# Routing and scattering tiles 0 to 15 during attention, into a slot region per expert, with unit slots fetched one by one

## The reference

```python
x = x + xattn(layernorm(x), ctx, Wq, Wk, Wv, Wo, bo)     # 16 heads of 64, 64 keys
# moe, on the 4096 rows xf = layernorm(x):
scores = softmax(xf @ gate_w.T)                          # 8 experts
_, idx = top_k(scores + gate_b, 2)
w = take_along_axis(scores, idx)                         # weight of each chosen expert
h = silu((xf @ w1[e] + b1[e]) * (xf @ w3[e] + b3[e]))    # hidden size 352
oe = h @ w2[e] + b2[e]                                   # per expert e
z = the same expert form with sw1, sw3, sw2              # shared expert, every row
x = x + sum_k w_k * oe[idx_k] + z
```

## Time and profile before

| | |
|---|---|
| median of 3 runs | 773.84 us |
| profiled execution, its own time | 774.89 us |
| its span | 773.1 us |
| TensorE busy | 673.9 us (87%) |
| VectorE / ScalarE / GpSimd busy | 535.4 / 396.8 / 426.0 us |
| granted TensorE clock, mean of the span | 0.951 |
| chain that ended last | PE 75%, DMA 12%, DVE 4%, POOL 4%, issue 3% |

### The profile page before, as it was taken

How to read it: one execution, slowest core, us unless ns; L and a number is a source line. 1 busy time by engine, 2 the same in 40 slices (tenths; PEclk the granted TensorE clock), 3 DMA queues, 4 the chain that set the end, 5 groups by cost and what they waited for, 6 DMA issues and landing times.

```text
span 773.1 us, 16281 instructions
## 1 busy us (share of the span) xinstructions
PE 673.9 (87%) x4635; PEld 633.5 (82%) x4636; DVE 535.4 (69%) x1053; ACT 396.8 (51%) x1287; POOL 426.0 (55%) x532
## 2 busy tenths in 40 slices
PE   4996899999999999486884049999999999999995
PEld 3784789999999998386884049999999999999994
DVE  3884888888888876586886016666666666666678
ACT  3995778778787774175331013443443443434432
POOL 5343765656656554124666743677677677676300
PEclk9997999999999999699998559999999999999998
DMA  8203342222222212599421012444444444446495
GB/s 233 75 1 109 103 151 89 79 73 70 70 71 81 69 49 68 148 328 297 119 72 50 1 51 46 77 72 69 76 72 71 78 68 72 77 88 103 86 385 238
DMA packets 65005, 79.96 MB, mean 103 GB/s; under 512 B 11337, under 2 KB 57906, under 8 KB 64946
## 3 DMA queue, kind: packets, MB, share of 16 engines
q1 hardware_dynamic: 47618, 55.81, 23.1%
q0 software_dynamic: 15744, 18.84, 15.5%
q10 hardware_dynamic: 1584, 4.59, 1.5%
HBM read 49.97 MB, written 29.24 MB: 102 GB/s over the span
## 4 chain that ended last, share of the span: by engine, by line
PE 75%; DMA 12%; DVE 4%; POOL 4%; issue 3%; ACT 1%; SPq 0%; ACTq 0%; POOLq 0%; DVEq 0%
PE ps L1094 62%; DMA slots_scratch<-record,slot 9%; POOL slots_scratch L626 4%; PE ps L1249 4%; PE ps L1177 3%; PE ps L1241 2%; PE ps L1154 2%; DMA wq_sb<-in_L_xattn_Wq 1%; DMA xrow<-xn_scratch,slots 1%; PE ps L1196 1%; PE ps L1167 1%; DVE hmax L864 0%; DVE sums L985 0%; PE ps L1113 0%; ACT prob L702 0%
## 5 line engine op out<-in xcount | busy, mean ns | idle before, releaser
L643 POOL DMA_INDIRECT acc_scratch<-yrow,slots x71 | 111.5, 1570 | 71.9 <-ACT yrow L804 70.8
L804 ACT ACTIVATE yrow<-ps,slots 128x256 f32<-128x256 f32 x71 | 33.7, 474 | 148.2 <-PE ps L1094 148.2
L626 POOL DMA_INDIRECT slots_scratch<-record,slot x64 | 66.1, 1032 | 63.1 <-DMA slots_scratch<-record,slot 34.8
L953 DVE TENSOR_TENSOR uxTl<-ps,uxTh 128x256 fp32r<-128x256 f32 x103 | 43.6, 423 | 79.2 <-ACT uxTh L814 78.6
L1094 PE MATMUL ps<-w13h,uxTh 128*128 x284 | 97.4, 343 | 0.0
L971 DVE TENSOR_TENSOR uv<-ps,b 128x704 f32<-128x704 f32 x71 | 63.3, 891 | 47.6 <-PE ps L1094 47.6
L814 ACT ACTIVATE uxTh<-ps 128x256 fp32r<-128x256 f32 x103 | 38.9, 378 | 106.3 <-PE ps L1241 88.4
L1094 PE MATMUL ps<-w13l,uxTh 128*128 x284 | 91.7, 323 | 0.0
L1094 PE MATMUL ps<-w13h,uxTl 128*128 x284 | 91.3, 321 | 0.0
L1241 PE MATMUL ps<-ident,xrow 128*128 128x128 f32 x206 | 40.6, 279 | 49.3 <-DMA xrow<-xn_scratch,slots 39.4
L636 POOL DMA_INDIRECT xrow<-xn_scratch,slots x71 | 69.5, 979 | 23.1 <-issue 20.7
(11 more groups left out here) (206 smaller groups left out, 2197.9 us busy)
## 6 DMA issues: line engine op xcount, KB each, us to landing
sums<-acc_scratch SPq DMA_DIRECT2D x16, 512.0 KB, 10.8
w_raw<-in_L_ffn_w SPq DMA_DIRECT2D x16, 352.0 KB
xin<-in_x SPq DMA_DIRECT2D x32, 128.0 KB, 2.5
acc_scratch<-yrow ACTq DMA_DIRECT2D x8, 512.0 KB, 2.7
xres<-in_x SPq DMA_DIRECT2D x32, 128.0 KB, 2.4
acc_scratch<-x SPq DMA_DIRECT2D x32, 128.0 KB, 1.9
xn_scratch<-xn SPq DMA_DIRECT2D x32, 128.0 KB, 2.4
xrow<-xn_scratch SPq DMA_DIRECT2D x32, 128.0 KB
```

Of the source, the lines that this page charges most:

```text
L626: pool.indirect_dma_start(slots_dram, bass.IndirectOffsetOnAxis(ap=slot[:, k, t:t + 1], axis=0), record[:, t, k, :], None).then_inc(scat_o ...
L643: pool.indirect_dma_start(acc_dram[u % 2], bass.IndirectOffsetOnAxis(ap=slots[:, u, 0:1], axis=0), yrow[:, m % YRING, :], None, compute_op ...
L804: act.activation(yrow[:, y, :], ps[:, 6 + m % 2, 0:D], ACT.Copy, scale=slots[:, bass.ds(u, 1), 1].bitcast(F32)).then_inc(y_ok, 1)
L953: dve.tensor_tensor(uxTl[:, p, :], ps[:, 0, 0:D], f32(uxTh[:, p, :]), ALU.subtract).then_inc(uxTl_ok, 1)
```

## The change

Routing is done in three groups: tiles 0 to 7, 8 to 15 (`GROUPS`) and 16 to 31 (`REST`). The new function `route(stage, ...)` holds the old chain cut in six stages. For the first two groups one stage is run by VectorE at the end of each of six attention steps (steps 14 to 19 and 22 to 27), with an Exp on ScalarE and nine small products on TensorE (`ranks`, in bank 0) between them. GpSimd scatters one tile's two record groups at the end of each attention step 20 to 35. Only tiles 16 to 31 are routed and scattered after attention.

So that a slot number can be given before the number of rows per expert is known, the table in HBM now has one region of 32 blocks of 128 slots per expert (`BLOCKS = 264`), the running count of each expert is kept in `carry`, and VectorE works out afterwards which block each unit has (`unit_row`). SyncE reads that number with `value_load` and fetches each unit's 128 slots by a DMA of its own (`unit_slots`): the first eight at s = 16 of its loop of the shared stage, behind a wait for all scatters, the other 63 behind the loop. The initial table is written during preparation, and ScalarE waits for it before its first write of A. The bias bo is folded into U by eight one-row products, so GpSimd's addition in each attention step is gone. The zeroing of `yrow` moves from the start to the end of preparation.

```diff
@@ SyncE
+            def unit_slots(u):
+                wait(sp, slots_in[u % RING], 16 * (u // RING))
+                row = sp.value_load(unit_row[0:1, u:u + 1], min_val=0, max_val=(BLOCKS - 1) * P)
+                sp.dma_start(slots[:, u, :], slots_dram[bass.ds(row, P), :]).then_inc(slots_in[u % RING], 16)
             for s in range(4, NA + LAG + 1):
+                if s == NA - 4:
+                    sp.wait_ge(eid_ok, 1)
+                    for half in scat_out:
+                        sp.wait_ge(half, 16 * NT)
+                    for u in range(RING):
+                        unit_slots(u)
...
+            for u in range(RING, NU):
+                unit_slots(u)
@@ GpSimd
-                t = s - 3
-                if has(t, NT):
-                    p = (par + 1) % 2
-                    wait(pool, xres_in[p], before(t) + 16)
-                    pool.tensor_tensor(xres[:, p, :], xres[:, p, :], bo_bc[:, :], ALU.add).then_inc(xb_ok, 1)
...
+            pool.memset(yrow[:, :, :], 0.0).then_inc(zero_ok, 1)
...
             def begin_step(s, par):
                 tile_step(s, par)
+                for g, (a, b) in enumerate(GROUPS):
+                    t = a + s - (b + 6 + STAGES)
+                    if a <= t < b:
+                        pool.wait_ge(slot_ok, g + 1)
+                        for k in range(TOP):
+                            scatter_record(t, k)
...
-            for t in range(NT):
+            pool.wait_ge(slot_ok, len(GROUPS) + 1)
+            for t in range(*REST):
                 for k in range(TOP):
...
             def gather(u):
                 m = (R0 + u) % RING
+                pool.wait_ge(slots_in[u % RING], 16 * (u // RING) + 16)
@@ ScalarE
                 elif kind == "A":
+                    if (j, i) == (0, 0):
+                        act.wait_ge(table_out, 16)
...
             def begin_step(s, par):
+                for g, (a, b) in enumerate(GROUPS):
+                    if s == b + 6 + 1:
+                        act.wait_ge(rt_sub, g + 1)
+                        act.activation(score[:, :, :], marked[:, 0, :, :], ACT.Exp).then_inc(rt_exp, 1)
                 tile_step(s, par)
@@ VectorE
+            def route(stage, g, a, b, marked, mark, score, biased, chosen, v, rank):
+                def best(k):
+                    link(dve.tensor_reduce(v[:, 3, :], biased, AX.X, ALU.max))
+                    link(dve.tensor_tensor(marked[:, 0, :, :], biased, over_e(v[:, 3, :]), ALU.is_ge))
+                    link(dve.tensor_tensor(marked[:, 0, :, :], marked[:, 0, :, :], over_t(pref[:, :]), ALU.mult))
+                    link(dve.tensor_reduce(v[:, 3, :], marked[:, 0, :, :], AX.X, ALU.max))
+                    link(dve.tensor_tensor(mark[:, k, :, :], marked[:, 0, :, :], over_e(v[:, 3, :]), ALU.is_equal))
+                if stage == 0:      # 2 instructions, then ScalarE's Exp
...
+                elif stage == 1:    # sum, reciprocal, scale, bias: 4
...
+                elif stage == 2:
+                    best(0)
+                elif stage == 3:
+                    link(dve.scalar_tensor_tensor(out=biased, in0=mark[:, 0, :, :], scalar=LOWEST, in1=biased,
+                                                  op0=ALU.mult, op1=ALU.add))
+                    best(1)
+                elif stage == 4:
+                    dve.tensor_tensor(chosen[:, 0:n, :], mark[:, 0, :, :], mark[:, 1, :, :], ALU.add).then_inc(chosen_ok, 1)
...
+                else:
+                    link(dve.tensor_tensor(biased, rank[:, 0:n, :], over_t(carry[:, :]), ALU.add))
+                    link(dve.tensor_tensor(carry[:, :], rank[:, n, :], carry[:, :], ALU.add))
+                    link(dve.tensor_tensor(marked, mark, biased.unsqueeze(1).to_broadcast([P, TOP, n, E]), ALU.mult))
+                    link(dve.tensor_reduce(v[:, 4:6, :], marked, AX.X, ALU.add))
+                    dve.tensor_copy(slot[:, :, a:b], v[:, 4:6, :]).then_inc(slot_ok, 1)
@@ TensorE
+            def ranks(bank, chosen, n):
+                pe.matmul(ps[:, bank, 0:(n + 1) * E], tri[:, :], chosen[:, :, :].rearrange("p t e -> p (t e)"), start=True, stop=False,
+                          skip_group_check=True)
+                for t in range(n):
+                    last = pe.matmul(ps[:, bank, (t + 1) * E:(n + 1) * E], ones[:, :], ...
...
+                for g, (a, b) in enumerate(GROUPS):
+                    if s == b + 6 + STAGES - 1:
+                        pe.wait_ge(chosen_ok, g + 1)
+                        pe.wait_ge(xTl_ok, s + 1)
+                        ranks(0, chosen, b - a).then_inc(rank_ok, 1)
```

More of the change, by code:

```diff
@@ L889, in tile_step @@
                     wait(dve, O_ok, t + 1)
-                    wait(dve, xb_ok, t + 1)
+                    wait(dve, xres_in[p], before(t) + 16)
                     wait(dve, x2_out[p], before(t))
@@ L938, in _, with begin_step @@
             dve.wait_ge(pre_act, NPRE)
-            steps(NT, 2, 6, tile_step, begun=0)
+            def begin_step(s, par):
+                tile_step(s, par)
+                for g, (a, b) in enumerate(GROUPS):
+                    stage = s - (b + 6)
+                    if stage == 0 and g == 0:
+                        dve.wait_ge(const_ok, 16)
+                    if stage == STAGES - 1:
+                        dve.wait_ge(rank_copied, g + 1)
+                    if 0 <= stage < STAGES:
+                        route(stage, g, a, b, marked[:, :, :, :], mark[:, :, :, :], score[:, :, :], biased[:, :, :],
+                              chosen[:, :, :], gv[:, :, :], rank[:, :, :])
+            dve.wait_ge(small_in, 80)
+            steps(NT, 2, 6, begin_step, begun=0)
             def unit_step(s, m, routed=None):
@@ L1032, in _ @@
-            dve.tensor_tensor(chosen[:, :, :], first[:, :, :], second[:, :, :], ALU.add).then_inc(chosen_ok, 1)
-            for k, mark in enumerate((first, second)):
-                link(dve.tensor_tensor(mA[:, :, :], mark[:, :, :], score[:, :, :], ALU.mult))
-                link(dve.tensor_reduce(record[:, :, k, 1].bitcast(F32), mA[:, :, :], AX.X, ALU.add))
-            dve.wait_ge(small_in, 96)
-            unit_step(0, 0)
-            dve.wait_ge(rank_ok, 1)
-            rows = v32[:, 4, 0:E]
@@ L1067, in _ @@
+            for stage in range(STAGES - 1):
+                rest(stage)
+            unit_step(0, 0)
+            dve.wait_ge(rank_ok, len(GROUPS) + 1)
+            rest(STAGES - 1)
             dve.wait_ge(hid_one, 2)
             unit_step(1, 1)
[L1070 to L1072 removed]
@@ L1073, in _ @@
-            link(dve.tensor_reduce(passed, big[:, :, :], AX.X, ALU.add))
+            rows, tiles, ends = (sums8[:, i, :] for i in range(3))
+            passed, begun, local, block_no = (units[:, i, :] for i in range(4))
+            link(dve.tensor_tensor(rows, carry[:, :], region[:, :], ALU.subtract))
+            link(dve.tensor_tensor(over_tile[:, :, :], rows.unsqueeze(2).to_broadcast([P, E, NT]),
+                                   tile128[:, :].unsqueeze(1).to_broadcast([P, E, NT]), ALU.is_gt))
@@ L1086, in _, with product @@
             PARTS = ((0, 0), (1, 0), (0, 1))
-            def product(out, stationary, moving, n):
+            def product(out, stationary, moving, n, more=False):
                 last = None
```

247 lines of the change are left out of this document (138 added, 109 removed).

## The result

| | median of the runs | runs | profiled execution |
|---|---|---|---|
| before, beside the changed kernel | 774.31 us | 772.53 to 775.34 (4) | 774.89, span 773.1 |
| changed | 781.92 us | 776.01 to 784.63 (4) | 776.01, span 774.3 |

The ratio is 1.0083 (95% interval 1.0051 to 1.0116): slower by 0.8%, where a gain of some 25 us, to 749 us, had been forecast. In a later group ten runs of the changed kernel gave 778.73 us, ratio 1.0054 (1.0025 to 1.0084). Ratios and their intervals leave out two executions in a slower state of the chip, one of 1049.2 us in the first edit of experiment 8 and one of 780.17 us in the second.

What follows compares the result with a forecast made beforehand. TensorE was taken to bound attention, routing and scatters the path after it. 774.89 - 37.5 (gap) + 10.2 (attention) + 2.1 (preparation) = 749.7, predicted as 749; range holding 8 of 10: 739 to 765 us.

Steps and rivals of the forecast that it cites:

- starting 5.8 us early gains about one pair: Behind attention: the 32 remaining scatters start 5.8 us earlier and have all landed at 400, before 419.9, so the gap goes.
- Rival 3: Late slots: scatters keep the first five's 2.98 us each, 32 end at 423, residual row 25 us late, 772; chance 0.14.
- attention's 12: Delay forecast up to the end of attention: 10.2 us in attention for two groups, 2.1 in preparation.
- SyncE's stall: Shared stage: eight fetches at 1.2 us from 400 delay tile 14's residual row, so VectorE waits 2.4 us; ends 0 and 27.5.
- Rival 2: GpSimd paces attention steps 20 to 35: slow scatters; x = 2.5 us each gives 799; chance 0.05 shared with another rival.
- The Exp: Attention, stage 0: ScalarE's Exp delays `xn2T`, so TensorE's gate products start 1.1 us late per group.
- the rank products: Attention: TensorE waits 1.8 us for `xTl`, then runs nine products at 0.114, 1.0 us; 2.8 per group.
- VectorE's stages beyond the slack: Attention, stages 1 to 5 on VectorE: what exceeds the slack delays the logits, 0.2 + 0.6 + 0.4 = 1.2 us per group.
- GpSimd's scatters: Attention: two scatters per step for 16 steps fit GpSimd's step, 7.2 of 7.41 us; cost 0, ends 0 and 18.
- preparation, taken at 2.1: Before attention: `yrow` zeroing +1.1 us, bo products +1.0, initial table and starting chain 0; sum 2.1.
- The bo products: Preparation: eight one-row products for bo at 0.12 each, +1.0 us.
- the wait for the first gathered rows: Before the routed units: TensorE's single wait of 39.2 us was to be gone; VectorE's idle of 37.1 us counted as gain.

Runs made afterwards that it cites:

- experiment 8: Changed kernel, two separate edits: first, all 64 scatters issued behind attention, 834.67 us; second, output bias bo left out, 775.15 us.
- experiment 1: Changed kernel with the slot table spread, neighbouring ranks 2.1 KB apart instead of 8 B: 755.94 us, ratio 0.9771 to the kernel before.
- experiment 3: Kernel before with a dense table, neighbouring ranks 8 B apart instead of 568 B: 812.30 us, ratio 1.0504.
- experiment 4: Kernel of experiment 6 with records inside each block of 128 rearranged, 64 B from rank to rank: 754.68 us, ratio 0.9738.
- experiment 6: Changed kernel with the first eight fetches issued by GpSimd behind its last scatter instead of SyncE: 772.90 us, ratio 0.9991.
- experiment 10: Changed kernel with spread table and GpSimd's first eight fetches, plus bo added by GpSimd during attention again: 752.20 us, ratio 0.9734.
- experiment 11: Changed kernel with spread table, GpSimd's first eight fetches, rank products moved to bank 5, and bo added by GpSimd: 743.82 us, ratio 0.9613.

## Why the prediction was wrong

- **The step that failed:** "starting 5.8 us early gains about one pair: all have landed when the 30th had before". It took the scatters' pace from the kernel before and looked only at when the loads beside them end. The change also moved where they write, from 568 B apart to 8 B apart, which the whole diff shows (the row-and-column split of the slot number is gone). The pace became 3.00 us instead of 2.16 a step, and the last scatter started at 434.1 instead of landing at 400; experiments 1, 3 and 4 show the distance as the cause, in both directions. Rival 3 named the result (2.98 each, 32 ended "at 423", or 435 with attention's 12; measured 434.1 plus the landing) but for another reason, and had 0.14. That its number fits is luck.
- **A term that wasn't there:** the dense scatters slow what runs beside them. From step 0 to 14 of the unit loop the five profiles of dense tables at the 32 KB pitch take 74.3 to 79.6 us, the six of spread ones 67.7 to 69.9; the kernel before took 65.2, its dense mirror 72.0. So of the 10.9 us in the ledger some 7 go with the dense table; some 3 to 4 stay with every variant. What is late are plain loads: VectorE's wait for the first residual row that holds it up, in the kernel before, its dense mirror, the changed kernel and the spread one:

```profile
365.73 0.42 DVE L947 TENSOR_TENSOR yrow<-ps,yrow 128x256 f32<-128x256 f32 x1 [5.20 <-DMA yrow<-acc_scratch]
```

```profile
371.07 0.42 DVE L947 TENSOR_TENSOR yrow<-ps,yrow 128x256 f32<-128x256 f32 x1 [10.94 <-DMA yrow<-acc_scratch]
```

```profile
387.43 0.42 DVE L1079 TENSOR_TENSOR yrow<-ps,yrow 128x256 f32<-128x256 f32 x1 [12.29 <-DMA yrow<-acc_scratch]
```

```profile
382.00 0.42 DVE L1083 TENSOR_TENSOR yrow<-ps,yrow 128x256 f32<-128x256 f32 x1 [7.66 <-DMA yrow<-acc_scratch]
```

  TensorE's longest wait for a shared row in this stretch goes the same way (4.7, 7.4, 10.1, 7.3 us). The Trainium skill, DMA: Bandwidth & Descriptors, section Back-pressure in remote DMA, says that stalled writes stall the other queues of the source DMA engine too. The loads' delay here agrees with it, though that section speaks of transfers between cores and no run here shows the stall itself.
- **SyncE's stall** was priced at 2.4 us with a landing at 400. The mechanism is as written (fetches 1.13 us each, forecast 1.2; then the residual row), but it starts at 437.4, where the forecast's 400 and attention's 12 make 412, and VectorE's wait is 17.3 us. Since gathered rows were late as well, taking SyncE out of its place gave only some 6 us (experiment 6).
- **Rivals.** Rival 3's time, 772, was short by 4 us for this profile; the delay of the loads was not in it. Rival 2's price at x = 2.5 is 2.8 us per step and not 3.1, by its own formula, which makes 794 and not 799; no scatter came near it.
- **Attention and preparation:** forecast 12.3, measured 14.1 at the last logits, of which attention alone is 9.8 for a forecast of 10.2. The parts were less good than the sum, so that part is luck. The Exp was to cost 1.1 us a group and let TensorE wait 0.51 and 0.87 in the two groups; the rank products were to wait 1.8 and take 1.0, and waited 1.49 and 1.63 and took some 0.25. The first group's:

```profile
204.63 0.19 PE L1232 MATMUL ps<-chosen,tri 128*128 128x72 bf16 x1 [1.49 <-DVE xTl L990]
204.66 0.35 PE L1235 MATMUL ps<-chosen,ones 128*128 128x64 bf16 x8
```

  The nine products aren't 0.114 each: it is 0.24 us from the first's start to the next product (204.87), for 72 columns and fewer instead of 248. The terms for VectorE's stages beyond the slack are 0.2 + 0.5 + 0.4 = 1.1 by the prediction's own figures, not 1.2. GpSimd's scatters, taken at 0, cost 1.4 to 3.0 us; preparation, taken at 2.1, cost 4.3, and 3 to 6 more in executions with the lower clock. The bo products are 1.7 us of it by their rows (0.43 us the pair, four times) instead of 1.0, though leaving them out gave back only 1.1. The cause of the rest stays open; in experiments 10 and 11, whose preparation has nothing of bo, the first row maximum is 1.3 and 0.6 us behind the kernel before (65.43).
- **Right:** the wait for the first gathered rows goes (to 0 by name); slots are ready 9.2 us after the last logits (340.47), where the forecast said 10.1 though its own terms add up to 9.8; routed units keep their pace (median 3.6 us). From step 20 to the last one the changed kernel gained 3.0 us, for 2.0 forecast.

## What to carry to other kernels

When a change moves what is scattered, work out the addresses as well as the count: keep neighbouring small records of one scatter apart (64 B was the least distance tried that stayed quick), and interleave the ranks inside a block if the block must stay contiguous for its reader. Take a DMA's pace only from rows that write in the same pattern. Before a queue is given a wait for something late, put the independent loads behind it in front, or give the wait to the queue that makes the late thing.

## What the runs showed of the hardware

- Scatters of 128 records of 8 B, behind attention and partly beside loads: 2.16 us a step with neighbours 568 B apart (30 steps), 2.33 at 2.1 KB, 2.42 at 64 B and 3.00 at 8 B (31 steps each). In the quiet, the last 19 steps of the kernel before took 1.27 each at 568 B, and the last 33 of its mirror 1.75 at 8 B.
- Scatters into adjacent records also delay plain loads on other queues: 14 steps of the unit loop took 7 us longer beside them, in the mirror of the kernel before as in the changed kernel.
- The granted clock fell to 0.65 to 0.73 in a 10 us window while TensorE was shown busy for 9.7 to 10.0 of it, in five of nine executions that have eight one-row products there (two for each of four batches, 0.43 us the pair), and in none of five without them; that the products are the cause isn't shown.
- A fetch of 1 KB at an address from a register, several in a row, took 1.13 us on SyncE and 1.15 on GpSimd from start to start.
